# Aggregating a graph layer by groups of four tiles, with the blocks written out and finished one late

## The reference, cut to what matters

```python
s2, d2, ea2 = _add_self_loops(src, dst, te, n)        # 50,000 edges and one self edge for each node
hx = (x @ Wg).reshape(n, h, f)                        # h*f = 256; h = 4 in layer 0, 1 in layer 1
al = jax.nn.leaky_relu(... [src] + ... [dst] + ...)
al = jnp.exp(al - m[dst])
al = al / jax.ops.segment_sum(al, dst, num_segments=n)[dst]
out = jax.ops.segment_sum(hx[src] * al[:, :, None], dst, num_segments=n)
```

## Time and profile before

| | |
|---|---|
| median of three runs | 4544.77 us (4540.06 to 4547.14) |
| the profiled execution's own time | 4547.42 us |
| its span, first to last instruction | 4545.9 us |
| `aggregate` of layer 0, first to last VectorE instruction | 1251.35 to 1783.2 us |
| `aggregate` of layer 1 | 2121.58 to 2596.7 us |

### The profile page before, as it was taken

How to read it: one execution, slowest core, us unless ns; L and a number is a source line. 1 busy time by engine, 2 the same in 40 slices (tenths; PEclk the granted TensorE clock), 3 DMA queues, 4 the chain that set the end, 5 groups by cost and what they waited for, 6 DMA issues and landing times. The chain is left out here.

```text
span 4545.9 us, 68833 instructions
## 1 busy us (share of the span) xinstructions
PE 2962.5 (65%) x16813; PEld 1910.2 (42%) x16939; DVE 2218.4 (49%) x5486; ACT 370.0 (8%) x793; POOL 977.4 (21%) x985
## 2 busy tenths in 40 slices
PE   1467677563066765602777628923999999989476
PEld 1133333352054454501555426712656565656345
DVE  7465656587356664712444420065444444444463
ACT  0211111100000000000000012212000000000131
POOL 0000000076367700566774020020000000000000
PEclk9888989876589898756999959966999999999797
DMA  1200000253134411623553153223121212121101
GB/s 60 69 29 36 32 32 32 103 194 118 30 107 119 116 27 54 204 65 111 140 140 93 59 202 125 101 65 135 57 94 57 93 57 93 57 94 57 37 0 40
DMA packets 206513, 378.78 MB, mean 83 GB/s; under 512 B 35807, under 2 KB 155344, under 8 KB 203222
## 3 DMA queue, kind: packets, MB, share of 16 engines
q1 hardware_dynamic: 120090, 188.27, 11.9%
q0 software_dynamic: 50384, 139.33, 10.9%
q10 hardware_dynamic: 35968, 50.35, 3.2%
HBM read 270.37 MB, written 108.29 MB: 83 GB/s over the span
## 5 line engine op out<-in xcount | busy, mean ns | idle before, releaser
L1850 PE MATMUL hop_wide<-hop_hs,counts 128*128 128x512 bf16 x3000 | 990.9, 381 | 35.0 <-DMA hop_hs<-hop_parts 35.0
L1851 PE MATMUL hop_narrow<-hop_hs,counts 128*128 128x256 bf16 x3125 | 855.8, 274 | 170.6 <-DMA hop_hs<-hop_parts 155.5
L653 POOL DMA_INDIRECT gat_ring<-hx_rows,src_i x784 | 793.4, 1012 | 339.3 <-issue 211.2
L1850 PEld LDWEIGHTS hop_wide<-hop_hs,counts 128*128 (+1 forms) x3125 | 307.1, 98 | 577.9 <-issue 215.5
L888 PE MATMUL cnt_acc<-cnt_oh_src,cnt_oh_dst 128*128 x1764 | 407.0, 367 | 137.3 <-issue 71.5
L1241 PE MATMUL agg_acc<-agg_msg,agg_oh 128*128 x880 | 278.3, 444 | 126.4 <-DVE agg_oh L1180 125.9
L888 PEld LDWEIGHTS cnt_acc<-cnt_oh_src,cnt_oh_dst 128*128 x1764 | 180.5, 102 | 350.8 <-issue 292.6
L1851 PEld LDWEIGHTS hop_narrow<-hop_hs,counts 128*128 (+1 forms) x3125 | 307.2, 98 | 36.4
L1823 DVE TENSOR_SCALAR hop_h<-hop_narrow,all_dis 128x256 f32<-128x256 f32 x125 | 60.5, 484 | 527.2 <-PE hop_narrow L1851 527.2
L1241 PE MATMUL agg_acc<-gat_ring,agg_oh 128*128 x880 | 258.4, 417 | 89.0 <-DVE agg_oh L1177 89.0
L848 DVE TENSOR_SCALAR cnt_oh_src<-cnt_number,cnt_column 128x1600 f16 x441 | 277.6, 629 | 0.0
(11 more groups left out here) (408 smaller groups left out, 3557.6 us busy)
## 6 DMA issues: line engine op xcount, KB each, us to landing
look_part<-src_low SPq DMA_DIRECT2D x28, 896.0 KB, 4.9
hop_hs<-hop_parts POOLq DMA_DIRECT2D x25, 960.0 KB, 8.1
hop_parts<-hop_parts SPq DMA_DIRECT2D x125, 192.0 KB, 1.9
count_rows<-cnt_out SPq DMA_DIRECT2D x50, 400.0 KB, 2.4
counts<-count_rows ACTq DMA_DIRECT2D x5, 4000.0 KB, 35.2
exp_w<-in_L_ffn_w SPq DMA_DIRECT2D x16, 1024.0 KB
hop_acc<-x_gcn SPq DMA_DIRECT2D x125, 128.0 KB, 2.0
x_gcn<-hop_acc SPq DMA_DIRECT2D x125, 128.0 KB, 1.8
```

The costliest lines, as they stand in the source:

```text
L653: pool.indirect_dma_start(out=self.ring[:, t % RING, :], out_offset=None, in_=self.g.hx_rows, in_offset=bass.IndirectOffsetOnAxis(ap=self. ...
L1850: pe.matmul(wide[i][:, :], count, hs[:, t, 0:2 * D], start=(t == 0), stop=(t == NB - 1))
L1851: mm = pe.matmul(narrow[i][:, 0:D], count, hs[:, t, 2 * D:3 * D], start=(t == 0), stop=(t == NB - 1))
```

## The change

Visits are by groups of four tiles (quads): 98 of them, so 98 + 24 = 122 visits, by a table `tile_quads`. In layer 0 one instruction weights four tiles (128x1040), and one comparison with a broadcast makes the matrices of two tiles (128x256). `oh[k]` holds two tiles, and TensorE multiplies four tiles in a visit, also those in which a block has no edge. `g.nodes` holds all 3,200 node numbers, made once for each layer by GpSimd ahead of the gathers in `edge_weights`. ScalarE scales the own rows by `w_self` into `looped`, and TensorE adds them as the product with the identity that opens the sums; in layer 0 ScalarE also does the maximum with zero (Relu). The loops over blocks are written out on VectorE, TensorE and ScalarE. Each engine loads only the last quad of a block, since the first is known; VectorE loads it between the two halves of the first visit. A block is finished after the loop of the next one (`finish(b - 1)`), with its own rows and residuals in three buffers, `y` and `looped` in two. The twelve products with zeros stay, and now stand ahead of the first visit. `aggregate` of layer 1 takes over the gathers from pair 58 on, where `edge_weights` had issued them up to 70. The diff, cut to its core; in the long functions below, the lines that go are those of the kernel printed above:

```diff
+QUADS, HELD = ET // 4, RING // 4
...
-                link(nc.vector.tensor_scalar(g.tile_pairs[:, :], g.tiles[:, :], 1, None, ALU.logical_shift_right))
-                link(nc.vector.tensor_scalar(g.minus_base[:, :], g.count[:, 0:NB], float(-P), None, ALU.mult))
+                link(nc.vector.tensor_scalar(g.tile_quads[:, :], g.tiles[:, :], 2, None, ALU.logical_shift_right))
...
-    AHEAD = ((60, 70, 70), (34, 42, 46))
+    AHEAD = ((60, 70, 70, 70), (34, 42, 46, 58))
...
-                pool.wait_ge(self.freed, after(q - RING // 2 + 1))
+                pool.wait_ge(self.freed, after(q // 2 - HELD + 1))
...
-            sp.sem_inc(self.in_order, 1)
+            if q % 2:
+                sp.sem_inc(self.in_order, 1)
...
+                pool.iota(g.nodes[:, :], pattern=[[1, NP]], base=0, channel_multiplier=0,
+                          allow_small_or_imprecise_dtypes=True)
                 g.gather.on_gpsimd(pool, g.gather.upto[1])
...
-                g.gather.on_gpsimd(pool, RING // 2)
+                g.gather.on_gpsimd(pool, g.gather.upto[3])
...
+    SLOTS3 = 3
...
+        ring = g.gather.ring[:, :, :].rearrange("p (q k) r -> p q (k r)", k=4)
+        in_order, freed = g.gather.in_order, g.gather.freed
+        oh = [s.sb(f"oh{k}", [P, 2, P]) for k in range(2)]
+        msg = None if layer else s.sb("msg", [P, 2, 4 * R])
+        own = [s.sb(f"own{i}", [P, ROW]) for i in range(SLOTS3)]
+        res = [s.sb(f"res{i}", [P, len(residuals), D]) for i in range(SLOTS3)]
+        looped, y, inv = ([s.sb(f"{n}{i}", [P, w]) for i in range(2)] for n, w in (("looped", R), ("y", D), ("inv", H)))
+        bias, zero = s.sb("bias", [P, D]), s.sb("zero", [P, P])
+        acc, idle = [s.ps(f"acc{i}") for i in range(2)], s.ps("idle")
...
+        def last_quad(eng, b):
+            return eng.value_load(g.tile_quads[0:1, b + 1:b + 2], min_val=0, max_val=QUADS - 1)
...
                 def load(b):
...
+                    i = b % SLOTS3
+                    act.dma_start(own[i][:, :], g.hx_rows[row_of(b), :]).then_inc(loaded[i], 16)
                     for n, src in enumerate(residuals):
...
+                        act.dma_start(res[i][:, n, :], src[row_of(b), :]).then_inc(loaded[i], 16)
+                def make_self(b):
+                    act.wait_ge(loaded[b % SLOTS3], after(16 * n_loads * (b // SLOTS3 + 1)))
+                    if b >= 2:
+                        act.wait_ge(summed, after(b - 1))
+                    for h in range(H):
+                        cols = slice(h * (F + 1), (h + 1) * (F + 1))
+                        act.activation(looped[b % 2][:, cols], own[b % SLOTS3][:, cols], ACT.Copy,
+                                       scale=g.w_self[:, b, h:h + 1]).then_inc(self_made, 1)
                 def store(b):
                     act.wait_ge(finished, after(b + 1))
...
+                    if not layer:
+                        act.activation(y[b % 2][:, :], y[b % 2][:, :], ACT.Relu).then_inc(turned_up, 1)
+                        act.wait_ge(turned_up, after(b + 1))
+                    act.dma_start(out_dram[row_of(b), :], y[b % 2][:, :]).then_inc(stored[b % 2], 16)
                 load(0)
...
+                for b in range(NB):
+                    make_self(b)
+                    if b >= 2:
+                        store(b - 2)
+                    if b + 1 < NB:
+                        if b >= 2:
+                            act.wait_ge(self_made, after(H * (b - 1)))
+                        load(b + 1)
+                store(NB - 2)
                 store(NB - 1)
...
+                for i in range(2):
+                    act.wait_ge(stored[i], after(16 * TURNS[i]))
...
+                def visit(q, b, frees, then=None):
+                    found = None
+                    dve.wait_ge(in_order, after(q + 1))
                     if not layer:
...
                         weighted = dve.tensor_tensor(
...
+                            at(msg, (q + b) % 2).rearrange("p (k f) -> p k f", f=F + 1),
+                            at(ring, q % HELD).rearrange("p (k f) -> p k f", f=F + 1),
+                            g.w_cols[:, bass.ds(4 * q, 4), 0:H].rearrange("p k h -> p (k h)").unsqueeze(2)
+                            .to_broadcast([P, 4 * H, F + 1]), ALU.mult)
                         if frees:
                             weighted.then_inc(freed, 1)
                     for k in range(2):
...
+                        dve.wait_ge(used[k], after(q + b))
                         if layer:
                             if frees and k == 1:
                                 dve.sem_inc(freed, 1)
...
+                            for n in range(2):
+                                tile = 4 * q + 2 * k + n
+                                hot = dve.tensor_scalar(oh[k][:, n, :], g.nodes[:, row_of(b)], at(g.dst_f, tile),
+                                                        at(g.w_cols, tile)[:, 0:1], ALU.is_equal, ALU.mult)
                         else:
...
+                            hot = dve.tensor_tensor(
+                                oh[k][:, :, :], g.nodes[:, row_of(b)].unsqueeze(1).to_broadcast([P, 2, P]),
+                                g.dst_f[:, bass.ds(4 * q + 2 * k, 2)].unsqueeze(2).to_broadcast([P, 2, P]), ALU.is_equal)
                         hot.then_inc(ready[k], 1)
...
+                        if then and not k:
+                            found = then()
+                    return found
+                def prepare(b):
+                    i = b % SLOTS3
+                    dve.wait_ge(loaded[i], after(16 * n_loads * (b // SLOTS3 + 1)))
+                    base = res[i][:, 0, :]
                     link(dve.tensor_tensor(base, base, bias[:, :], ALU.add))
                     for n in range(1, len(residuals)):
...
+                        link(dve.tensor_tensor(base, base, res[i][:, n, :], ALU.add))
+                def finish(b):
+                    i = b % 2
+                    base = res[b % SLOTS3][:, 0, :]
+                    sums = heads(acc[i][:, 0:R])
                     dve.wait_ge(summed, after(b + 1))
...
+                    dve.wait_ge(stored[i], after(16 * (b // 2)))
+                    link(dve.reciprocal(inv[i][:, :], sums[:, :, F]))
                     if layer:
...
+                        dve.scalar_tensor_tensor(y[i][:, :], acc[i][:, 0:D], inv[i][:, 0:1], base, ALU.mult,
+                                                 ALU.add).then_inc(finished, 1)
+                        dve.wait_ge(finished, after(b + 1))
+                        dve.sem_inc(read, 1)
                     else:
...
+                        link(dve.tensor_tensor(heads(y[i][:, :]), sums[:, :, 0:F],
+                                               inv[i][:, :].unsqueeze(2).to_broadcast([P, H, F]), ALU.mult))
+                        dve.sem_inc(read, 1)
+                        dve.tensor_tensor(y[i][:, :], y[i][:, :], base, ALU.add).then_inc(finished, 1)
+                first = 0
+                last = visit(first, 0, False, lambda: last_quad(dve, 0))
+                for b in range(NB):
+                    prepare(b)
+                    with dve.If(last > first):
+                        with dve.Fori(first + 1, last + 1) as q:
+                            visit(q, b, True)
+                    if b:
+                        finish(b - 1)
+                    if b + 1 < NB:
+                        first, last = last, visit(last, b + 1, False, lambda: last_quad(dve, b + 1))
+                finish(NB - 1)
...
+                pe.wait_ge(zeroed, after(1))
+                first = 0
+                for b in range(NB):
+                    sums = acc[b % 2][:, 0:R]
+                    if b >= 2:
+                        pe.wait_ge(read, after(b - 1))
+                    pe.wait_ge(self_made, after(H * (b + 1)))
+                    pe.matmul(sums, g.ident[:, :], looped[b % 2][:, :], start=True, stop=False, skip_group_check=True)
+                    last = last_quad(pe, b)
+                    for _ in range(12):
+                        pe.matmul(idle[:, 0:P], zero[:, :], zero[:, :], start=True, stop=True)
+                    with pe.Fori(first, last + 1) as q:
+                        rows = at(ring, q % HELD) if layer else at(msg, (q + b) % 2)
                         for k in range(2):
...
+                            pe.wait_ge(ready[k], after(q + b + 1))
+                            for n in range(2):
+                                t = (2 * k + n) * (ROW if layer else R)
+                                mm = pe.matmul(sums, oh[k][:, n, :], rows[:, t:t + R], start=False, stop=False,
+                                               skip_group_check=True)
+                            mm.then_inc(used[k], 1)
+                    pe.matmul(acc[b % 2][:, 0:1], zero[:, :], zero[:, 0:1], start=False, stop=True,
                               skip_group_check=True).then_inc(summed, 1)
+                    first = last
```

(63 more changed lines are left out.)

47 lines of the change are left out of this document (7 added, 40 removed).

## The result

The changed kernel takes 4255.51 us (median of four runs, 4251.9 to 4259.36) against 4544.41 for the kernel before on the same chip: a ratio of 0.9365 (95% interval 0.9349 to 0.9381), 289 us less. The forecast was 4310, so the direction and the range held and the likeliest value was 54 us too careful.

What follows compares the result with a forecast made beforehand. The prediction took the VectorE-TensorE hand-over to bound both aggregations. From 4547.4 us, it took off 123 (layer 0), 84 (layer 1) and 29 (gathers): 4311, in the runs' median 4309, rounded to 4310; range 4240 to 4410.

Steps and rivals of the forecast that it cites:

- Bound and structure: Both aggregations: no engine is full; VectorE and TensorE limit the stages by handing over to each other.
- The forecast case: Whole kernel: shorter visits and boundaries in both aggregations and fewer gathers in edge_weights give 4310 us; chance 0.76.
- rival (1): Both aggregations: boundaries vanish and gathers bound, stages shrink to 325 and 353 us, total 4186 us; chance 0.08.
- Visits of layer 0: Layer 0 aggregation: a visit takes 2.49 us for four tiles, against 3.32; 122 visits are 304 us.
- Boundary of layer 0: Between layer 0 blocks: TensorE's first visit starts at T + 6.4, VectorE's second half ends at T + 8.9 us.
- T: In both aggregations, the moment at which VectorE has made the last matrix of a block.
- Supply of layer 0: Layer 0 aggregation: 252 gathers at 1.25 us each need 315 of 409 us, so GpSimd does not bind.
- the circle of 2.26 us: Layer 1 visit: product, release, new matrices and signal in turn take 2.26 us for four tiles; 122 visits are 276.
- Gathers: edge_weights of layer 1: 24 gathers fewer save 30 us, the iota ahead costs 0.9; -29 us.
- ScalarE and the late finish at zero: Both aggregations: ScalarE's work, own-row loads and the `read` signal given with the finish stay hidden; priced at zero.
- rival (2): Entries of written-out loops: one 2.93 us code stall more in each of 50 blocks, +147, total 4457 us; chance 0.12.
- (3): Small loops' backward jumps wait for code: gain gone at 1.2 us a jump, 4780 us at twice that; chance 0.04.

Runs made afterwards that it cites:

- the halved supply: Changed kernel, but from pair 70 on only the first tile of each pair is gathered, old rows standing for the others: 4225.53 us, ratio 0.9285.
- b_blocks_written: Kernel before with only the loops over blocks written out on VectorE, TensorE and ScalarE, visits still by pairs: 4485.32 us, ratio 0.9856.
- the second group: Four single edits of the changed kernel on a second chip (zeros out, narrow comparison, finish on time, gathers back): ratios 0.9478, 0.9465, 0.9571, 0.9573 to the kernel before.

## Why the prediction was right, and what was mis-sized

**Bound and structure: right.** The stages stayed limited by the hand-over between VectorE and TensorE, and the gain came stage by stage. The forecast case is what happened in most blocks; rival (1) is what happened at the end of layer 0. That the sum came within 54 us owes something to luck: in layer 0 two errors of opposite sign stand in it.

**Visits of layer 0.** The durations were right to 1%. Starts of the weighting are not 2.5 us apart but uneven (1.9 to 3.7). A block of five visits takes 14.65 us. By the forecast's own terms it would take 8.9 + 3 x 2.49 = 16.4; its 16.1 is the mean over 22 such blocks and three with four visits.

**Boundary of layer 0: too dear by 1.9 us.** From T the forecast had the last product end at 1.7, the closing one at 1.9, the identity at 2.5, a load to 3.0 and zeros to 6.4. Measured: closing ends at 1.4, identity at 2.0, no visible load, and the visit starts at 4.5. TensorE's queue reads the bound while products are still running, so the 0.5 of the load was hidden. The zeros took 2.84, the best value, not the 3.4 mean of before: that mean came from stages at clock 0.91 and 0.95, and this one ran at 0.97. VectorE's second half ends at T + 7.0 (1307.39) instead of 8.9; the 7.65 us that remain of a block are three visits of 2.55, not 2.49. Net 1.7 us a block, some 43 over 25 blocks.

**Supply of layer 0: missed.** The step "in layer 0 the supply needs 315 of 409 us" took the gathers' pitch from the edge weights, 1.25 us. In the stage itself it was already 1.36 before (252 gathers from 1258.7 to 1599.2), or 1.32 without the short waits for a free place in the ring, and is 1.48 now. From 1571.84 us on VectorE waits for landings, and three of the last four blocks take 20.2, 22.5 and 23.1 us instead of 14.65; the halved supply prices this at 23 us. The two errors have opposite signs: 409 - 43 + 23 = 389, measured 390.

**Layer 1: the circle of 2.26 us was too long by 0.1 to 0.2, the boundary by 1.5.** VectorE remakes a buffer within TensorE's other half, so the visit is TensorE's own 2.0 to 2.16. The boundary shrank for the reasons of layer 0. A block of five visits takes 13.8 us instead of 8.9 + 3 x 2.26 = 15.7, which is 48 us over 25 blocks. Some 11 are lost again, so that 353.6 is 37 under the forecast 391. Half of them lie at the start, where the first product waits for the own rows and their scaling and the zeros behind it take 5.2 us at a granted clock of 0.51; 4 lie in the last block but one, which waits for gathers. That rival (1) gave 353 is a coincidence: the halved supply frees only 6 us, while TensorE is 98% busy.

**Gathers: right**, -29 forecast, -28 here and alone. The iota took 2.80 us as estimated. The wait behind GpSimd's last gather, taken as 8.6 us on both sides of the sum, was 8.7 before and 9.8 with the gathers moved alone.

**ScalarE and the late finish at zero: consistent**, not isolated. After the first block no product with the identity waits for ScalarE.

**Rivals (2) and (3): not seen on the chip of the result.** VectorE's idle time put down to issue is 16.9 us in 42 places of layer 0 (longest 0.5) and 11.2 in 27 of layer 1 (longest 0.6). The rule of the Trainium skill, page "Runtime: NRT & Kernel Launch", section "Instruction fetch mechanics", allowed a stall at the jumps; in these two stages the trace shows none, and b_blocks_written, with loops in 25 places too, gained 65 us. On the chip of the second group idle times of up to 7.2 us do stand ahead of a block's first visits, so for such a chip rival (2) stays open.

## What to carry to other kernels

Take the pace of a supply from the stage that it must feed, with the neighbours that it will have there, not from a quiet stretch: whether the same gather takes 1.25 or 1.48 us decided 23 us. When a part tried alone gives the forecast gain, look still where in the stage it lies: the gain here was forecast for the visits and came mostly at the boundaries. When two engines that hand over are both relieved, work out who is third, and compare the whole stage with that engine's total; halving its work is a cheap experiment that prices it. Filler, such as the products with zeros, is free or dear by what stands behind it: the same twelve products cost nothing while the gathers bound and 58 to 66 us once they did not.

## What the runs showed of the hardware

A VectorE multiplication of 128x1040 32-bit numbers delays an indirect DMA issued by GpSimd in its course by about 0.46 us. A register load on TensorE's queue took 0.30 us and left no gap behind queued products. Between GpSimd's last gather and the first instruction behind the barrier there were 10.3 us here, by these two rows (8.7 in the kernel before):

```profile
1940.94 0.94 POOL L653 DMA_INDIRECT gat_ring<-hx_rows,src_i  x1 [0.30 <-issue]
...
1952.15 0.17 DVE L1179 MEMSET agg_zero<- 128x128 f32 x1 [14.03 <-SPq L664]
```

And one of the chips ran the kernel before 10% slower than the others; on it the changed kernels show stretches of single TensorE instructions 1.40 us apart.
